# Two graph layers on one core: joined first stage, other chunks in the middle and at the end, another order inside a pair of groups

## The chip, the cores and the metric

The kernel runs on one core of one Trainium2 chip. The metric is the device time of one launch in microseconds (us). A core has a matrix engine (PE), a vector engine (DVE), an activation engine (ACT), GpSimd (POOL), which here mainly issues gathers and scatters by index, and SyncE (SP), which here only issues plain transfers. They run their own instruction lists and meet by semaphores.

## The reference

N = 3125 nodes with 256 features, E = 50000 edges sorted by `dst`, 128 features and one weight for each edge. Cut to what matters:

```python
h = concat(x[src], x[dst])                       # layer 0, an MLP on each edge
h = tanh(h @ W0 + b0); h = tanh(h @ W1 + b1); h = h @ W2 + b2
h = h * (edge_attr @ Wg)
x = layernorm(x + segment_sum(h, src) / max(segment_count(src), 1))

h = einsum('ni,hio->hno', x, W)                  # layer 1, 4 heads of 64
e = leaky_relu(a_src.h[src] + a_dst.h[dst], 0.2) * edge_weight
p = exp(e - max(e)); alpha = p / (segment_sum(p, dst)[dst] + 1e-10)
x = layernorm(x + segment_sum(h[src] * alpha, dst))
```

## The kernel before

Nodes lie in 25 tiles of 128. Edges lie in 391 blocks of 128, 98 groups of 4 blocks and 49 pairs of 2 groups. Since edges are sorted by `dst`, the receivers of a group lie in one window of 128 nodes. Products of the first layer are made of a high and a low part, three matmuls for each (L1420 to L1422). The launch has five stages, and the semaphores and the order in which each engine's function is written set the order of everything.

**First stage.** PE makes x·W0 for 25 "sender" tiles and then 25 "receiver" tiles (`node_part`, 6 matmuls each, 8 banks). DVE adds the bias to a sender tile into the ring `stA` of 4 slots (L573), and SP stores it to the table TA in HBM (L1164). For a receiver tile ACT copies the high part into the ring `stB` (L1698), DVE writes the low part (L539), and SP stores both to TB (L1169). A sender tile has 203 KB, a receiver tile 406 KB. POOL gathers rows of TA when all of TA is written. Between the sender tiles DVE makes the low parts of the weights. `wait_stage_n0` lets DVE, ACT and SP go on when all products are made and all stores have landed. Then SP loads the receiver rows of windows 0 and 1 (`load_window`: `rel`, then TW out of TB in two halves), DVE clears some constants (L721 to L725) and makes the first one-hot matrix (`window_hot`, L647).

**Group loop.** For each of the 98 groups PE runs the whole edge MLP and the sums of a block's edges by sender; ACT does tanh and copies; DVE low parts and one-hot matrices; POOL gathers TA and adds rows to four tables accA in HBM (L1316). At each step SP issues window g+2, then `ef` (edge features) and `bcast_i` (sender numbers) of g.

**Middle.** When the adds have landed (`wait_stage_a`), SP loads the four tables in five chunks of 5 tiles (`tab`, two buffers). DVE sums them and makes the mean, the residual and the statistics (`mean_residual`), ACT takes the root and normalises (`deviations`, `normalise`), PE transposes and multiplies by the weights Wc, whose last columns are a product of WcT and `ablk` (L1567). ACT copies a tile's result in two parts, `node` and `hst` (L1698). SP stores `hst` to HT and `node` to DT. Behind the chunks DVE makes tables for the next stage (L810 to L828, `in_tile` among them), then waits for the last `node`.

**Pair loop.** POOL gathers rows of HT into `Hg` (L1351), 4 for a group, into a ring of 12 groups. For a pair q of two groups the work is: `edge_scores` (L875 to L897; it waits for the gathers and for PE's `destination_scores`, semaphore s_ad), `spread_maxima` (PE, L1617), `running_maximum` (L904, L908), `weighted_rows` for each group (L913, writes `xb` and frees 4 slots of `Hg`), `window_sums` for each (PE, L1628), `carry_window` (L944), `window_rows` (L860), `one_hot` (L851) and `destination_scores` (PE, 24 matmuls L1608). One turn of PE's loop before:

```python
window_sums(2 * q)
window_sums(2 * q + 1)
spread_maxima(q + 2)
destination_scores(q + 3)
```

**End.** 25 gathers by POOL bring a node's sums (`fin`). DVE and ACT do residual, statistics and normalisation in five chunks, and SP stores each tile.

Of the kernel before, what the change touches and what calls it, by code (L numbers as in the profile page):

```python
# [6 lines left out]
P = 128  # L7
# [10 lines left out]
def build_program(nc, xT, x, src_cols, dst_cols, src_row, dst_row, eT, w_cols,  # L18
# [37 lines left out]
    TC = 5  # L56
    NC = -(-NT // TC)
# [44 lines left out]
    with ctx:  # L102
# [45 lines left out]
        eps = sb("eps", [P, 1])  # L148
        zeros = sb("zeros", [P, BW])

# [17 lines left out]
        b1c = sb("b1c", [P, C2], f32, sa)  # L168
        sn = ExitStack()
# [8 lines left out]
        stA = sb("stA", [P, N0R, H0], f32, sn)  # L178
        stB = sb("stB", [P, N0R, 2, H0], f32r, sn)
# [8 lines left out]
        rel_b = sb("rel_b", [NG, GE], bf16, sn)  # L188
        W1f = sb("W1f", [P, C1, HC], f32, sn)
# [11 lines left out]
        h1s = sb("h1s", [KS, 2, GE], f32r, sa)  # L201
# [6 lines left out]
        gate = sb("gate", [P, 2, 2, OUT], f32, sa)  # L208
        mf = sb("mf", [P, 2, 2, OUT], f32, sa)
# [3 lines left out]
        EQR = 3 * BLOCKS_PER_GROUP  # L213
        eqA = sb("eqA", [P, EQR, P], f32r, sa)
        eq_low = sb("eq_low", [P, 2, P], bf16, sa)
# [17 lines left out]
        outside = sb("outside", [1, 1], i32, sc)  # L233
        in_tile = sb("in_tile", [P, NG, NT], bf16, sc)
        reached = sb("reached", [P, NT, NG], bf16, sc)
# [23 lines left out]
        TSR = 2  # L259
# [3 lines left out]
        WcT = sb("WcT", [P, DK, OUT], f32, s1)  # L263
        ablk = sb("ablk", [P, DK, 2 * HEADS], f32, s1)
        hst = sb("hst", [P, 4, BW], f32, s1)
# [123 lines left out]
        s_ldc = sem("s_ldc")  # L389
        s_tab = [sem(f"s_tab{i}") for i in range(TSR)]  # L390
# [38 lines left out]
        s_st = sem("s_st")  # L429
# [28 lines left out]

        def part_cols(i):
            return slice(i * tiles_per_part * P, min((i + 1) * tiles_per_part * P, N))  # L460
# [18 lines left out]
        def wait_stage_n0(eng):  # L479
# [4 lines left out]
            eng.wait_ge(s_rd, 16 * RDS)  # L484
            eng.wait_ge(s_pad, 16)
            eng.wait_ge(s_wl, 4)
# [6 lines left out]
        def tiles_of_chunk(c):  # L493
            return range(c * TC, min((c + 1) * TC, NT))

# [31 lines left out]
        def _(dve):  # L527
# [35 lines left out]
            def receiver_lo(t):  # L563
                n = rows_of_tile(t)
                dve.wait_ge(s_n0b, t + 1)
                lo(stB[0:n, t % N0R, 1, :], bank_n0(NT + t)[0:n, 0:H0], stB[0:n, t % N0R, 0, :]).then_inc(s_n0l, 1)

            def sender_bias(t):
                n = rows_of_tile(t)
                dve.wait_ge(s_n0, t + 1)  # L570
                if t >= N0R:
                    dve.wait_ge(s_ta[t % N0R], 16 * (t // N0R))
                dve.tensor_tensor(stA[0:n, t % N0R, :], bank_n0(t)[0:n, 0:H0], b0b[0:n, :], ALU.add)\  # L573
# [26 lines left out]
            for t in range(4):  # L600
                sender_bias(t)
# [3 lines left out]
            const(dve.tensor_scalar(low2_i[:, :, :], low_all[:, 2:4, :], 2.0, None, ALU.mult), "low_i")  # L605
# [6 lines left out]
            for t in range(4, NT):  # L612
                sender_bias(t)
                if t == 10:
# [3 lines left out]
                if t == 13:  # L618
# [9 lines left out]
                if t == 16:  # L628
                    dve.wait_ge(s_wh, 4)
                    lo(Wgl[:, :], Wgf[:, :], Wgh[:, :]).then_inc(s_wl, 1)  # L630
                if t == 20:
# [6 lines left out]
            for t in range(NT):  # L638
                receiver_lo(t)
# [80 lines left out]
            wait_stage_n0(dve)  # L720
            const(dve.memset(h2l[2 * Q:P, :, 2, :].bitcast(f32), 1.0))  # L721
            const(dve.memset(mh[:, :, :, OUT:OUT + 1].bitcast(f32), 1.0))
            const(dve.memset(mh[:, :, :, OUT + 1:AW].bitcast(f32), 0.0))
            const(dve.memset(h1s[:, :, :].bitcast(f32), 0.0))
            const(dve.memset(ml[:, :, :, OUT:AW].bitcast(f32), 0.0), "ones")  # L725

            for s in range(-2, NG + 1):
# [41 lines left out]
            def mean_residual(c):  # L769
# [5 lines left out]
                dve.tensor_tensor(rows[:, 0], rows[:, 0], rows[:, 1], ALU.add).then_inc(s_sum, 1)  # L775
                dve.wait_ge(s_sum, c + 1)
# [21 lines left out]
            wait_stage_a(dve)  # L798
            const(dve.memset(ablk[:, :, :], 0.0), "ablk")
            const(dve.memset(node[:, :, :], 0.0), "node clear")  # L800
            dve.wait_ge(s_xn, 48)
            for c in range(NC):
                mean_residual(c)
                if c >= 1:
                    norm_factors(c - 1, c - 1)
            norm_factors(NC - 1, NC - 1)

# [16 lines left out]
            const(dve.scalar_tensor_tensor(worst[:, 2:3], worst[:, 1:2], float(P), worst[:, 0:1], ALU.mult, ALU.max))  # L824
            const(dve.tensor_scalar(outside[:, :], worst[0:1, 2:3], float(P), None, ALU.is_ge), "outside")
            const(dve.memset(neg_m[:, 0:1], -LOWEST), "no maximum")
            if rows_of_block(NB - 1) < P:
                const(dve.memset(score[:, NB - 1, :], LOWEST))  # L828
            dve.wait_ge(s_hc, NT)
            const(dve.tensor_copy(iota_p, iota_row[:, :]))  # L830
# [132 lines left out]
            for q in range(-3, NQ + 1):  # L963
# [14 lines left out]
                if q + 3 < NQ:  # L978
                    one_hot(q + 3)
# [20 lines left out]
            with if_outside(dve):  # L1000
# [8 lines left out]
                dve.wait_ge(s_st, 32)  # L1009
# [77 lines left out]
            def attention_residual(c):  # L1087
# [23 lines left out]
                last.then_inc(s_att, 1)  # L1111
# [851 lines left out]
```

## Time and profile before

| | us |
|---|---|
| median of 3 runs | 2435.32 (2430.52 to 2443.21) |
| the profiled execution | 2453.26 |
| its span, first to last instruction | 2451.1 |

The profile is of one execution, 18 us above the median. Busy time is the time in which an engine works on an instruction; PE and its weight loads (PEld) overlap. Numbers in front of a row are us from the span's start. `[14.03 <-remote]` behind a row is the idle time of the engine before it and what ended that; "remote" is a releaser that the profile can't name.

### The profile page before, as it was taken

To read this page: it belongs to the slowest core of one execution; us is meant where nothing else is said; L and a number is where in the kernel's file an instruction comes from. 1 tells how busy PE (TensorE), PEld (TensorE's weight loads), DVE (VectorE), ACT (ScalarE), POOL (GpSimd) and SP (SyncE) were. 2 spreads that over 40 slices of the span, in tenths; PEclk is the share of its full clock that TensorE was granted. 3 is DMA by queue.
4 is the path that set the end of the run, shared out by engine and by line. 5 is a ranking of instruction groups with operands and counts; after the bars stand their busy time and mean duration, and the time that the engine had idled before them with its cause. 6 is when DMAs were issued, how large, how long until landed. Compare 5 with 4: busy or idle time off the path is not lost. (4 is left out here: it accounts for less than half of the span.)

```text
span 2451.1 us, 40398 instructions
## 1 busy us (share of the span) xinstructions
PE 1929.3 (79%) x12892; PEld 1704.4 (70%) x12892; DVE 1509.6 (62%) x3750; ACT 1382.8 (56%) x2780; POOL 1470.6 (60%) x1204
## 2 busy tenths in 40 slices
PE   7699999999999999999999999955134545544560
PEld 6588899988999999999999999954123333433440
DVE  6466666666666666666666666645155445444575
ACT  2488888888888888888888888845000000000012
POOL 0317778777777777767777777532645645654623
PEclk9899999999999999999999999977567667766785
DMA  5878877777777777777777777665434434444523
GB/s 198 287 204 182 196 165 169 170 166 166 160 160 158 159 159 159 157 161 154 158 159 158 158 158 159 131 158 138 107 87 120 129 106 123 129 110 109 134 83 108
DMA packets 236167, 370.81 MB, mean 151 GB/s; under 512 B 35853, under 2 KB 168935, under 8 KB 235949
## 3 DMA queue, kind: packets, MB, share of 16 engines
q0 software_dynamic: 101232, 188.20, 38.7%
q1 hardware_dynamic: 134717, 179.94, 24.4%
q8 instruction: 107, 1.75, 0.3%
q14 instruction: 111, 0.91, 0.1%
HBM read 270.57 MB, written 97.45 MB: 150 GB/s over the span
## 5 line engine op out<-in xcount | busy, mean ns | idle before, releaser
L1316 POOL DMA_INDIRECT accA<-ystage,to_a x391 | 650.2, 1663 | 231.0 <-issue 108.0
L1322 POOL DMA_INDIRECT GA<-TA,src_c x391 | 425.1, 1087 | 328.7 <-issue 93.3
L1351 POOL DMA_INDIRECT Hg<-HT,src_c x391 | 371.1, 949 | 346.0 <-DVE xb L913 168.7
L1861 ACT ACTIVATE drop<-neg_m 128x1 f32<-128x1 f32 x49 | 14.5, 295 | 627.3 <-DVE neg_m L908 517.1
L1420 PE MATMUL bank<-h1h,W1h 128*128 128x512 f32 x882 | 349.2, 396 | 1.3 <-DVE h1l L539 0.7
L1422 PE MATMUL bank<-h1h,W1l 128*128 128x512 f32 x882 | 348.0, 395 | 0.0
L1421 PE MATMUL bank<-h1l,W1h 128*128 128x512 f32 x882 | 347.0, 393 | 0.0
L539 DVE TENSOR_TENSOR h2l<-h2f,h2h 128x512 fp32r<-128x512 f32 (+1 forms) x294 | 202.8, 690 | 202.4 <-issue 87.3
L1628 PE MATMUL bank<-xb,in_window 128*128 128x260 f32 (+1 forms) x782 | 249.7, 475 | 70.3 <-issue 69.2
L539 DVE TENSOR_TENSOR h1l<-h1f,h1h 128x512 fp32r<-128x512 f32 x294 | 194.9, 690 | 131.2 <-ACT h1h L1698 112.9
L1628 PEld LDWEIGHTS bank<-xb,in_window 128*128 128x128 f32 (+1 forms) x782 | 182.4, 241 | 122.4 <-issue 87.3
L1698 ACT ACTIVATE mh<-mf 128x512 fp32r<-128x512 f32 x196 | 123.9, 632 | 207.5 <-DVE mf L676 195.1
L1617 PE MATMUL bank<-diag,ones 128*128 128x128 f32 x98 | 27.5, 371 | 249.5 <-DVE diag L897 180.1
L1421 PE MATMUL bank<-W2l,h2h 128*128 128x256 f32 (+1 forms) x782 | 220.9, 282 | 0.0
L1420 PE MATMUL bank<-W2h,h2h 128*128 128x256 f32 (+1 forms) x782 | 219.7, 281 | 0.4 <-DVE mf L676 0.4
L1422 PE MATMUL bank<-W2h,h2l 128*128 128x256 f32 (+1 forms) x782 | 219.4, 281 | 0.0
L1729 ACT ACTIVATE h1f<-bank 128x512 f32<-128x512 f32 (+1 forms) x392 | 206.9, 584 | 10.1 <-PE bank L1472 10.1
L1754 ACT ACTIVATE h2f<-bank,b1c 128x512 f32<-128x512 f32 x294 | 201.9, 687 | 6.7 <-issue 1.3
L1617 PEld LDWEIGHTS bank<-diag,ones 128*128 128x128 f32 x98 | 20.7, 239 | 261.3 <-DVE diag L897 188.3
L1422 PEld LDWEIGHTS bank<-h1h,W1l 128*128 128x128 f32 x882 | 165.8, 188 | 39.3
L1420 PEld LDWEIGHTS bank<-h1h,W1h 128*128 128x128 f32 x882 | 166.5, 189 | 36.6 <-DVE h1l L539 3.4
L875 DVE TENSOR_TENSOR score<-Hg,bank 128x32 f32<-128x32 f32 (+2 forms) x50 | 9.0, 182 | 295.4 <-remote 286.4
(209 smaller groups left out, 5235.1 us busy)
## 6 DMA issues: line engine op xcount, KB each, us to landing
TW<-TB SPq DMA_DIRECT2D x196, 203.0 KB
ef<-in_eT SPq DMA_DIRECT2D x97, 256.0 KB
bcast_i<-in_src_row SPq DMA_DIRECT2D x97, 256.0 KB
HB<-hist SPq DMA_DIRECT2D x98, 130.0 KB
rel<-RL SPq DMA_DIRECT2D x97, 128.0 KB
rem<-RD SPq DMA_DIRECT2D x48, 256.0 KB
TB<-stB SPq DMA_DIRECT2D x24, 406.0 KB
accA<-zeros SPq DMA_DIRECT2D x4, 1677.0 KB, 13.0
```

The lines of the kernel that those rows point to most:

```text
L539: return dve.tensor_tensor(o, full, hi.bitcast(f32), ALU.subtract)
L1316: return pool.indirect_dma_start(out=table, out_offset=bass.IndirectOffsetOnAxis(ap=rows, axis=0), in_=sums, in_offset=None, compute_op=AL ...
L1322: pool.indirect_dma_start(out=GA[0:n, b % (GAR * BLOCKS_PER_GROUP), :].bitcast(f32), out_offset=None, in_=TA, in_offset=bass.IndirectOffse ...
L1351: pool.indirect_dma_start(out=Hg[0:n, slot, :], out_offset=None, in_=HT, in_offset=bass.IndirectOffsetOnAxis(ap=src_c[0:n, b:b + 1], axis= ...
L1420: pe.matmul(o, lh, rh, start=first, stop=False)
L1421: pe.matmul(o, lh, rl, start=False, stop=False)
L1422: return pe.matmul(o, ll, rh, start=False, stop=last)
L1617: pe.matmul(PTOP[:, 0:P], ones[:, :], diag[:, q % 2, :], start=True, stop=True).then_inc(s_sp, 1)
L1628: last = pe.matmul(PS[g % 3][:, 0:BW], in_window[0:n, j, :], xb[0:n, j, :], start=b == blocks[0], stop=b == blocks[-1])
L1698: return act.activation(o, i, ACT.Copy)
L1729: act.activation(h1f[0:k1(c), c, 0:n], PT[u % 2][0:k1(c), 0:n], ACT.Tanh).then_inc(s_tanh1, 1)
L1754: act.activation(h2f[:, m, 0:n], PL1[u % 2][:, 0:n], ACT.Tanh, bias=b1c[:, m:m + 1]).then_inc(s_tanh2, 1)
```

## The change

**First stage.** A list `STEPS` mixes the tiles: at each 7 steps two receivers to five senders until the senders are done (25 senders and 10 receivers in the first 35 steps), then the other 15 receivers. PE, DVE, ACT and SP follow it. SP loads window 0 behind step 35, once the first ten receiver tiles have landed, and window 1 behind step 37; the rows that these two windows ask for are clamped to the first ten tiles, and a test at the end covers other inputs. The wait for the stores leaves the start of the group loop: DVE and ACT pass it at s = 1, SP ahead of window 2.

**Group loop.** SP issues `ef` and `bcast_i` of g ahead of window g+2. At g = 14 it loads WcT and `ablk`.

**Middle and end.** Chunks of 3, 5, 5, 5, 5 and 2 tiles; three buffers `tab`; `in_tile` and the other tables ahead of the chunks; the product WcT·ablk right behind the group loop; ACT's table of the root loaded ahead of the wait (`warm`); 20 matmuls of `ident` on PE when the first tables land; `hst` takes all 264 columns and POOL copies `node` out of it (25 copies), no store to DT; the factors of chunk c-1 are made inside chunk c; ACT takes the roots of c+1 behind two thirds of a chunk in the middle, and at the end behind the normalisation of c.

**Pair loop.** `edge_scores(q + 2)` and `spread_maxima(q + 2)` move between the pair's two groups, and `one_hot` ahead of `window_rows`.

```diff
+        EARLY = 10
+        steps_s, steps_r, STEPS = [], [], []
+        while len(STEPS) < 2 * NT:
+            sender = len(steps_s) < NT and len(STEPS) % 7 not in (1, 4)
+            (steps_s if sender else steps_r).append(len(STEPS))
+            STEPS.append(("sender" if sender else "receiver", len(steps_s if sender else steps_r) - 1))
...
-            wait_stage_n0(dve)
...
-            for s in range(-2, NG + 1):
+            window_hot(0)
+            wait_products_n0(dve)
+            const(dve.memset(h2l[2 * Q:P, :, 2, :].bitcast(f32), 1.0), "ones")
+            const(dve.memset(ablk[:, :, :], 0.0), "ablk")
+
+            for s in range(-1, NG + 1):
+                if s == 1:
+                    wait_stores_n0(dve)
...
-            wait_stage_n0(sp)
-            load_window(0)
-            load_window(1)
+                if p == 35:
+
+                    for k in range(N0R):
+                        sp.wait_ge(s_tb[k], early_stores(k))
+                    sp.wait_ge(s_xl, PARTS)
+                    sp.wait_ge(s_rd, 16 * RDS)
+                    load_window(0)
+                if p == 37:
+                    load_window(1)
+            wait_products_n0(sp)
             for g in range(NG):
                 n = edges_of_group(g)
-                if g + 2 < NG:
-                    load_window(g + 2)
...
+                if g + 2 < NG:
+                    load_window(g + 2)
...
-    TC = 5
-    NC = -(-NT // TC)
+
+    CHUNKS = [range(a, b) for a, b in zip((0, 3, 8, 13, 18, 23), (3, 8, 13, 18, 23, NT))]
...
-            copy(node[0:n, t, :], bank[t % 4][0:n, BW:BW + HEADS])
-            copy(hst[0:n, t % 4, :], bank[t % 4][0:n, 0:BW]).then_inc(s_hc, 1)
+                act.wait_ge(s_nd, t - 3)
+            copy(hst[0:n, t % 4, :], bank[t % 4][0:n, 0:BW + HEADS]).then_inc(s_hc, 1)
...
+            pe.wait_ge(s_tab[0], chunk_arrivals(0))
+            for _ in range(20):
+                pe.matmul(bank[3][:, 0:P], ident[:, :], ident[:, :], start=True, stop=True)
...
+                if 0 <= q + 2 < NQ:
+                    edge_scores(q + 2)
                 if 0 <= q < NQ:
                     weighted_rows(2 * q + 1)
                 if 0 <= q - 1:
                     carry_window(2 * q - 1)
-                if 0 <= q + 2 < NQ:
-                    edge_scores(q + 2)
+                if q + 3 < NQ:
+                    one_hot(q + 3)
```

On PE in the pair loop, from the third turn on, before:

```order
L1628 MATMUL bank<-xb,in_window 128x260 x8
L1617 MATMUL bank<-diag,ones 128x128
L1608 MATMUL bank<-ad_p,hot 128x4 x24
L1628 MATMUL bank<-xb,in_window 128x260 x8
L1617 MATMUL bank<-diag,ones 128x128
```

and now (L1694 is the line that was L1628, L1683 was L1617, L1674 was L1608):

```order
L1694 MATMUL bank<-xb,in_window 128x260 x4
L1683 MATMUL bank<-diag,ones 128x128
L1694 MATMUL bank<-xb,in_window 128x260 x4
L1674 MATMUL bank<-ad_p,hot 128x4 x24
L1694 MATMUL bank<-xb,in_window 128x260 x4
```

The maxima's matmul stands between the two groups' sums; the destination scores stay behind the second.

On DVE in the same loop, from a pair's first `weighted_rows` on, before:

```order
L913 TENSOR_TENSOR xb<-Hg,bank3 128x4x256
L932 TENSOR_TENSOR drop_k<-drop,keep 128x1
L944 SCALAR_TENSOR_TENSOR hist<-hist,drop_k,bank7 128x260
L904 TENSOR_REDUCE top_g<-bank1 128x1
L908 SCALAR_TENSOR_TENSOR neg_m<-top_g,neg_m 128x1
L913 TENSOR_TENSOR xb<-Hg,bank3 128x4x256
L944 SCALAR_TENSOR_TENSOR hist<-hist,keep,bank5 128x260
L875 TENSOR_TENSOR score<-Hg,bank0 128x32
L883 SCALAR_TENSOR_TENSOR score<-score 128x32
L889 TENSOR_TENSOR score<-score,w_c 128x32
L892 TENSOR_REDUCE top_c<-score 128x1
L897 TENSOR_SCALAR diag<-ident,top_c 128x128
```

and now (L958 was L913, L920 to L942 were L875 to L897, L896 was L851, L905 was L860):

```order
L958 TENSOR_TENSOR xb<-Hg,bank3 128x4x256
L977 TENSOR_TENSOR drop_k<-drop,keep 128x1
L989 SCALAR_TENSOR_TENSOR hist<-hist,drop_k,bank5 128x260
L949 TENSOR_REDUCE top_g<-bank1 128x1
L953 SCALAR_TENSOR_TENSOR neg_m<-top_g,neg_m 128x1
L920 TENSOR_TENSOR score<-Hg,bank0 128x32
L928 SCALAR_TENSOR_TENSOR score<-score 128x32
L934 TENSOR_TENSOR score<-score,w_c 128x32
L937 TENSOR_REDUCE top_c<-score 128x1
L942 TENSOR_SCALAR diag<-ident,top_c 128x128
L958 TENSOR_TENSOR xb<-Hg,bank3 128x4x256
L989 SCALAR_TENSOR_TENSOR hist<-hist,keep,bank6 128x260
```

The five score instructions stand ahead of the second `xb` instead of behind its carry.

On SP behind the row stores of the first stage, before:

```order
L1158 DMA RL<-rel_b 1x336
L1164 DMA TA<-stA 128x406 x24
L1164 DMA TA<-stA 48x406
L1164 DMA TA<-stA 5x406
L1169 DMA TB<-stB 128x812 x24
L1169 DMA TB<-stB 48x812
L1169 DMA TB<-stB 5x812
L1182 DMA rel<-RL 128x512
```

and now, at the end of the mixed tiles (L1228 stores senders, L1232 receivers, L1215 and L1221 load a window):

```order
L1228 DMA TA<-stA 5x406
L1232 DMA TB<-stB 128x812
L1215 DMA rel<-RL 128x512
L1218 TENSOR_LOAD low_i
L1218 ISA x2
L1221 ISA
L1221 DMA TW<-TB 128x406
```

The first window's loads stand 14 receiver tiles ahead of the end of the stores.

## Rows read from the trace of the kernel before

**Rows 1.** The page: busy time, share of the span, instructions.
```profile
PE 1929.3 (79%) x12892; PEld 1704.4 (70%) x12892; DVE 1509.6 (62%) x3750; ACT 1382.8 (56%) x2780; POOL 1470.6 (60%) x1204
```

**Rows 2.** Windows, group loop and pair loop: from:to, length, busy by engine (instructions), clock, DMA share, GB/s.
```profile
104.40:1608.00 1503.60, 1500.69 (x10245) 1360.69 (x10246) 1033.38 (x2617) 1259.64 (x2421) 1044.22 (x756) 1.00 0.74 163
1698.60:2387.00 688.40, 308.74 (x2053) 238.14 (x2053) 334.49 (x745) 38.63 (x153) 371.10 (x391) 0.69 0.43 114
```

**Rows 3.** Windows inside the first stage, same columns.
```profile
30.00:60.00 30.00, 27.32 (x138) 25.96 (x136) 20.18 (x42) 6.20 (x14) 0.00 (x0) 0.94 0.50 177
60.00:95.00 35.00, 25.62 (x118) 22.85 (x117) 11.99 (x21) 10.17 (x20) 15.31 (x16) 0.90 0.97 354
```

**Rows 4.** First stage, waits of ACT, 30 to 105 us: total, times, longest.
```profile
ACT stB L1698 <- DMA TB<-stB: 14.0, 13, 4.2
```

**Rows 5.** First stage, timeline of DVE and PE.
```profile
99.46 0.91 DVE L721 MEMSET h2l<- 64x1024 f32 x1 [3.13 <-DMA TB<-stB]
104.38 0.79 PE L1472 MATMUL bank<-hot,TW 128*128 128x256 f32 x2 [13.62 <-DMA TW<-TB]
```

**Rows 6.** Group loop, timeline of SP's queue and DVE.
```profile
820.78 0.42 SPq L1182 DMA_DIRECT2D rel<-RL  x1
823.82 0.55 DVE L647 TENSOR_SCALAR hot<-rel,half_f 128x512 fp32r<-128x512 bf16 x1
```

**Rows 7.** Middle, timeline of DVE, PE, ACT and POOL.
```profile
1644.67 1.50 DVE L775 TENSOR_TENSOR tab<-tab 128x1290 f32<-128x1290 f32 x1 [6.14 <-DMA tab<-accA]
1647.87 0.60 SPq L1228 DMA_DIRECT2D ablk<-in_a_dst  x1
1651.96 1.85 PE L1567 MATMUL bank<-ablk,WcT 128*128 128x8 f32 x8 [25.61 <-DMA ablk<-in_a_dst]
1655.42 0.30 ACT L1831 ACTIVATE std<-mv,eps 128x5 f32<-128x5 f32 x1
1696.10 0.17 ACT L1698 ACTIVATE node<-bank 53x4 f32<-53x4 f32 x1 [0.57 <-PE bank L1588]
1696.17 0.37 ACT L1698 ACTIVATE hst<-bank 53x260 f32<-53x260 f32 x1
1698.62 1.02 POOL L1351 DMA_INDIRECT Hg<-HT,src_c  x1 [62.31 <-DMA HT<-hst]
```

**Rows 8.** Pair loop, 1698.6 to 2387 us: waits of DVE and POOL.
```profile
DVE score L875 <- remote: 286.4, 22, 47.3
POOL Hg L1351 <- DVE xb L913: 168.7, 23, 16.1
```

**Rows 9.** Pair loop, timeline of DVE, POOL and PE around one restart.
```profile
2017.90 0.19 DVE L875 TENSOR_TENSOR score<-Hg,bank 128x32 f32<-128x32 f32 x1 [14.03 <-remote]
2020.52 1.21 DVE L913 TENSOR_TENSOR xb<-Hg,bank 128x1024 f32<-128x1024 f32 x1
2022.00 0.94 POOL L1351 DMA_INDIRECT Hg<-HT,src_c  x1 [7.33 <-DVE xb L913]
2028.54 0.75 PE L1608 MATMUL bank<-ad_p,hot 128*128 128x4 bf16 x24
2040.73 0.95 POOL L1351 DMA_INDIRECT Hg<-HT,src_c  x1 [0.30 <-issue]
2044.89 0.19 DVE L875 TENSOR_TENSOR score<-Hg,bank 128x32 f32<-128x32 f32 x1 [14.04 <-remote]
```

**Rows 10.** Pair loop, timeline of PE and DVE where POOL does not pause.
```profile
1884.14 0.19 DVE L875 TENSOR_TENSOR score<-Hg,bank 128x32 f32<-128x32 f32 x1 [14.04 <-remote]
1893.41 0.75 PE L1608 MATMUL bank<-ad_p,hot 128*128 128x4 bf16 x24
1905.12 0.19 DVE L875 TENSOR_TENSOR score<-Hg,bank 128x32 f32<-128x32 f32 x1 [3.84 <-remote]
1969.68 0.18 DVE L875 TENSOR_TENSOR score<-Hg,bank 128x32 f32<-128x32 f32 x1
```

**Rows 11.** End, timeline of ACT.
```profile
2443.92 5.02 ACT L1837 ACTIVATE xn<-xn,shift,rstd 128x256 f32<-128x256 f32 x10
```

More of the change, by code:

```diff
@@ L262, in build_program @@
         x1T = sb("x1T", [P, XTR, DK, P], f32, s1)
-        WcT = sb("WcT", [P, DK, OUT], f32, s1)
-        ablk = sb("ablk", [P, DK, 2 * HEADS], f32, s1)
-        hst = sb("hst", [P, 4, BW], f32, s1)
+        hst = sb("hst", [P, 4, BW + HEADS], f32, s1)
         s1.close()
@@ L457, in build_program, with early_stores @@
         part_of_tile = [t // tiles_per_part for t in range(NT)]
+        EARLY = 10
[4 more added lines that the diff above has]
+            STEPS.append(("sender" if sender else "receiver", len(steps_s if sender else steps_r) - 1))
+        def early_stores(slot):
+            return 16 * sum(len(pieces(t)) for t in range(slot, EARLY, N0R))
         def part_cols(i):
@@ L493, in tiles_of_chunk @@
         def tiles_of_chunk(c):
[L494 removed]
+            return CHUNKS[c]
         def load_tables(eng, chunks):
@@ L599, in _, with staged @@
             dve.wait_ge(s_b0, 16)
-            for t in range(4):
-                sender_bias(t)
+            def staged(p):
+                kind, t = STEPS[p]
+                if kind == "sender":
+                    sender_bias(t)
+                else:
+                    receiver_lo(t)
+            for p in range(4):
+                staged(p)
             dve.wait_ge(s_lowp, 1)
@@ L796, in norm_factors @@
                     .then_inc(s_shift, 1)
[L798 to L806, printed above, removed]
+            dve.wait_ge(s_Yc, NB)
             low = low_all[:, 0, :]
@@ L828, in _ @@
                 const(dve.memset(score[:, NB - 1, :], LOWEST))
+            wait_stage_a(dve)
+            const(dve.memset(node[:, :, :], 0.0), "node clear")
+            dve.wait_ge(s_xn, 48)
+            for c in range(NC):
+                mean_residual(c)
+            norm_factors(NC - 1, NC - 1)
             dve.wait_ge(s_hc, NT)
+            dve.wait_ge(s_nd, NT)
             const(dve.tensor_copy(iota_p, iota_row[:, :]))
@@ L1205, in _ @@
                              src_row[g * GE:g * GE + n].partition_broadcast(P)).then_inc(s_bc[g % 2], 16)
+                if g == 0:
+                    for k in range(N0R):
+                        sp.wait_ge(s_tb[k], stores(N0R, k))
+                    sp.wait_ge(s_pad, 16)
+                if g + 2 < NG:
+                    load_window(g + 2)
                 if g in (2, 3):
@@ L1353, in gather_h_rows @@
                     in_offset=bass.IndirectOffsetOnAxis(ap=src_c[0:n, b:b + 1], axis=0)).then_inc(landed, 16)
+            pool.wait_ge(s_dc, DC["node clear"])
+            for t in range(NT):
+                n = rows_of_tile(t)
+                pool.wait_ge(s_hc, t + 1)
+                pool.tensor_copy(node[0:n, t, :], hst[0:n, t % 4, BW:BW + HEADS]).then_inc(s_nd, 1)
+            pool.wait_ge(s_nd, NT)
             for k in range(4):
@@ L1425, in node_part @@
             def node_part(u):
-                t, half = u % NT, u // NT
+                kind, t = STEPS[u]
+                half = 0 if kind == "sender" else 1
                 n = rows_of_tile(t)
@@ L1704, in _, with receiver_hi @@
                 copy(xTh[:, :, part_cols(i)], xTf[:, :, part_cols(i)]).then_inc(s_xh, 1)
+            def receiver_hi(t):
+                n = rows_of_tile(t)
+                act.wait_ge(s_n0, steps_r[t] + 1)
+                if t >= N0R:
+                    act.wait_ge(s_tb[t % N0R], 16 * (t // N0R))
+                copy(stB[0:n, t % N0R, 0, :], bank_n0(steps_r[t])[0:n, 0:H0]).then_inc(s_n0b, 1)
+            for t in range(6):
+                receiver_hi(t)
             act.wait_ge(s_ldw, 16 * (C1 + 2 * 2 + 2 * 3 + 2 + 2 + 1))
@@ L1716, in _ @@
             copy(Wgh[:, :], Wgf[:, :]).then_inc(s_wh, 1)
[L1717 to L1722 removed]
+            for t in range(6, NT):
+                receiver_hi(t)
             def tanh1(g, c):
```

193 lines of the change are left out of this document (104 added, 89 removed).

## The prediction

> **What bounds the kernel now.** The page's busy shares [rows 1] name no single engine: PE is busy for 79% of the span, POOL 60%, DVE 62%. So the windows come next [rows 2], and then, stage by stage, the table of waits and the timeline around the longest of them. In the group loop PE is busy 1500.7 of 1503.6 us at full clock: PE alone sets 61% of the span, and nothing that the change does to the other engines there can gain. The other stages have 947 us. In the longest of them, the pair loop, the busiest engine (POOL) works 371 of 688 us. There engines wait for each other, and the waits are what the change can move. The times below are differences of stages in the profiled execution (2453.3 us, of which 2451.1 is span). That run lies 18 us above the median, which no stage owns visibly, so I take the sum of the differences off the median, 2435.3. What a measurement of this kernel can tell from no change is about 0.5%, 12 us.
>
> **First stage.** The transfers are the bound, unevenly: from 30 to 60 us, the senders' half, they move 177 GB/s at a DMA share of 0.50, and from 60 to 95 us 354 GB/s at 0.97 [rows 3]. There ACT waits 14 us for slots of `stB` [rows 4]. Behind it stands a tail: stores landed at 99.46, windows loaded, PE's first matmul of the loop at 104.38 after 13.6 us of idleness [rows 5].
> Mixing the tiles fills the first half. 30 x 177 + 35 x 354 KB per us = 17.7 MB; all at 354 GB/s is 50 us, so 15 us less. PE allows it: 138 matmuls in 27.3 us [rows 3] are 0.198 us each, a step of six 1.19 us, 50 steps 59 us; with the first at about 22 they end near 82. Last low part then about 84, h2l's clearing 0.9 (the other clearings of 99.46 to 102 move off the path), and PE starts the group near 87 to 90. Window 0 is loaded 15 steps, some 18 us, earlier; only the wait for all stores (now ahead of window 2, first needed two groups or 30 us later) stays, hidden by PE's two groups. The gain by the end of the products is 104.4 - 88.5 = 16; by the transfers 15. Against: POOL's gathers of TA start later, since the last sender is now step 34 instead of 24, and share the transfers with the last receivers. Bounds: 10 (the first gathers late by 5 us) to 19. I take **-15**.
>
> **Group loop.** PE's work is the same, so **0**. The one thing that moves towards the path is `rel`: SP issued it a turn (15 us) earlier, and now issues it behind `bcast_i`, which waits for DVE's duplicates. In the old trace that place is 820.78, and `window_hot` used it at 823.82 [rows 6]: 3.0 us, 0.42 of it the issue. DVE has 31% of idle time in this loop [rows 2], so a microsecond's delay is absorbed; above that it costs up to 1 us x 96 groups. WcT and `ablk`, nine loads of 0.60 us each in SP's queue [rows 7] (one stands there), now delay one turn of SP by about 6 us, once; a turn lasts 15.3 us (1503.6 / 98) and the loads then behind them are due a turn later.
>
> **Middle.** The first root stands at 1655.42, though DVE started on the tables at 1644.67: ACT had to wait for the product of Wc, and that for `ablk`, the last of whose eight loads SP queued at 1647.87: the product ran from 1651.96 for 1.85 us [rows 7]. With both made during the group loop and a first chunk of three tiles (3/5 of the table bytes and of the statistics; my estimate for these, from the sum's 1.50 us for five tiles, is 4 us from the sum's start to the root instead of 6) the first root comes near 1648: -7.5. From there to the last `hst` (1696.54) are 41.1 us for 25 tiles. Dropping `node` (0.07 us until `hst` starts, 0.17 by its own duration [rows 7]) gives 2 to 4 us, a last chunk of two tiles and the later place of the roots 1 or 2 more. POOL's 25 copies run beside ACT; ACT's pace is 41.1/25 = 1.64 us a tile, and only a copy slower than that would show: at 2 us, 25 x 0.36 = +9. `in_tile` and its neighbours now precede the chunks, while the last adds and the tables are under way: DVE waited 6.14 us for the tables alone [rows 7], about what they take, so nothing either way. The store to DT stood behind the last `hst`, on no path. The 20 dummy matmuls stand where PE waits. Sum **-12**, bounds -3 and -16.
>
> **End.** ACT's last piece normalises ten tiles, 5.02 us [rows 11]; the root of the last chunk stood ahead of the normalisation of the one before. With two tiles left it is 2 x 0.5: -4. The first chunk of three can start up to 2 gathers (2.5 us) earlier, of which I count 1. **-5**, bounds -2 and -8.
>
> **Pair loop.** 688 us, 14.0 a pair. POOL's own work is 371 us [rows 2], so it isn't the bound; it waits 169 us for `xb`, and DVE waits 286 us in 22 pieces ahead of `edge_scores` for something the profile calls remote [rows 8]. Around one piece [rows 9]: restart of DVE at R = 2017.90, two `xb` free the ring, POOL restarts at 2022.00 and issues 16 gathers without a pause, the last at 2040.73 for 0.95 us, DVE restarts at 2044.89. A ring of 12 groups has the gathers landed long before. What `edge_scores` otherwise waits for is s_ad, the signal of PE's destination scores. Those ran at 2028.54, for 0.75 us, and DVE went on only 15.6 us later, 3.2 us behind the end of POOL's row of gathers. So I read: **signals of PE are held back while POOL issues gathers in a long row.** The cycle is 27.0 us for two pairs: 4.1 (R to POOL) + 19.7 (16 gathers) + 3.2.
> The change alters both ends. After R DVE does the scores (1.1 us) and then at once the second `xb` (1.21), instead of scores, `window_rows` (1.22), `one_hot`, `xb` [rows 9]: POOL restarts at about R + 2.5, 1.6 earlier. If still two pairs fit in a cycle, it is 25.4 us. 18 cycles of 27.0 us are 486 of the 688 us; the rest is the start (one wait of 47.3 us [rows 8]), the stretch of rows 10 and the end. So 18 x 1.6 = -29, bounds 0 and -35 (22 waits).
> But PE's destination scores of the next pair now stand behind the second group's sums, which need that second `xb`: R + 2.3, 8 matmuls of L1628, about 3.3 (an estimate: PE's 308.7 us of the stage [rows 2] are 6.3 us a pair, most of it the sums of two groups), and 0.75 for the scores: R + 6.3, nearly 4 us into POOL's row. Before they were done ahead of POOL's restart, and their signal passed. Rows 10 show one such case: scores at 1893.41 in the middle of a row, DVE's restart at 1905.12.
> The Trainium skill (SBUF — State Buffer, the section on SBUF's two separate sides) says that only the port pair shared by DVE and GpSimd causes contention, and that PE and ACT never wait for anyone. By that rule nothing holds PE's signals; it would give rival D's second value, 2235. The trace speaks against it: in the 14.04 us ahead of 2044.89 DVE is idle and has no port to share, and still the signal doesn't come.
>
> **Rivals.**
> (A) Two pairs per cycle, restart earlier, all terms as above: -15 - 12 - 5 - 29 = -61, **2374**. For it: the mechanism's first half is read off directly. Chance 0.36.
> (B) The pair loop doesn't change, since the signal is released at a fixed time of its own: -32, 2403. Chance 0.17.
> (C) The signal is held at every pair: only two `xb` are free in a cycle, so POOL has 8 gathers: 2.5 + 9.7 + 3.2 = 15.4 us a pair instead of 13.5, times 48 is +91, in all 2494; with the 11 us of rows 10 now and then only, +30, 2433. It is slower than before from about 14.2 us a pair on. For it: rows 10. Against: in the stretch from 1884.14 to 1969.68 [rows 10], where POOL hardly pauses and such cases occur, seven pairs took 85.5 us, 12.2 each. Chance 0.24, 0.14 of it slower than before.
> (D) That stretch's 12.2 us a pair become the rule, since POOL no longer pauses: -1.3 x 48 = -62, 2341; with no signal held at all POOL is the bound, 8 x 1.25 = 10 us a pair (the 16 gathers of rows 9 in 19.7 us), -3.5 x 48 = -168, 2235. Chance 0.18, nearly all at the first value.
> (E) `rel` comes late in the group loop, +0.5 to +1 us each, or the mixed stage loses what it wins: 2435 to 2480. Chance 0.05.
>
> **How the numbers follow.** The likeliest is A, 2374. The range leaves out the worst half of C and of E and the tail of D: 2325 to 2450. Faster by over 0.5% (below 2423): A, B, D and 0.06 of C and E, 0.77. Within: 0.07. Slower (above 2447): 0.16.
>
> **What would show it.** First stage: PE's first one-hot matmul (was L1472) near 88, and a DMA share near 1 from 35 us on; if it is at 95 or later, the gathers of TA were late. Group loop: 1503 us long, no wait for `rel`. Middle: the first root 4 us behind the start of the first table sum instead of 11, and POOL's first gather of `Hg` 12 us nearer to the group loop's end. Pair loop: DVE's remote waits still about 22 with POOL's restart 2.5 us behind each (A); about 45 waits, each after 8 gathers (C); few waits and PE's scores passing during the row (D). End: last normalisation of two tiles. The forecast is wrong if the held signals turn out to be something else, such as gathers that land late: then the order inside a pair decides nothing, and B comes.

## The result, and the profile after

The changed kernel takes 2396.57 us (median of 4 runs, 2395.63 to 2399.12); the kernel before 2432.92 us (4 runs, 2429.91 to 2443.21). The ratio is 0.9855, with a 95% interval of 0.9832 to 0.9878: 36 us faster, inside the stated range, where 61 us were forecast. The profiled run of after took 2397.3 us, next to its median, while that of before lay 18 us above its own. A stage's difference between these two profiles is therefore too large, and a second profile of before (2431.96 us, span 2429.7) stands beside them in this table. Its columns are the start of PE's group loop, the loop to POOL's last add, from there to the first gather of `Hg`, from there to the first gather of `fin`, and the rest.

| kernel | loop starts | group loop | middle | pair loop | end |
|---|---|---|---|---|---|
| before | 104.4 | 1530.5 | 63.8 | 696.1 | 56.3 |
| before, second profile | 102.8 | 1526.1 | 62.9 | 682.5 | 55.4 |
| after | 94.5 | 1523.9 | 57.6 | 664.3 | 55.4 |

Against the second profile the stages give -8.3, -2.2, -5.3, -18.2 and 0: 34 us, about the difference of the medians. The forecast had -15, 0, -12, -29 and -5. No stage got slower; each gain but the group loop's was overrated.

The windows of after by stage, with the columns of [rows 2]:

```profile
94.50:1608.00 1513.50, 1512.25 (x10365) 1378.79 (x10365) 1040.58 (x2648) 1266.58 (x2446) 1049.10 (x761) 1.00 0.74 164
1676.00:2340.30 664.30, 336.36 (x2053) 255.73 (x2053) 341.03 (x746) 38.85 (x153) 374.85 (x392) 0.71 0.46 118
```

PE still fills the group loop (its idleness fell from 2.9 to 1.3 us), and the pair loop is still one in which everyone waits.

**First stage**, timeline of ACT, DVE and PE, in order of engine; the last row answers to the last of [rows 5]:

```profile
73.34 0.51 ACT L1765 ACTIVATE stB<-bank 128x406 fp32r<-128x406 f32 x1 [5.95 <-DMA TB<-stB]
80.70 0.51 ACT L1765 ACTIVATE stB<-bank 128x406 fp32r<-128x406 f32 x1 [5.86 <-DMA TB<-stB]
...
93.41 0.57 DVE L563 TENSOR_TENSOR stB<-bank,stB 53x406 fp32r<-53x406 f32 x1 [1.04 <-ACT stB L1765]
93.91 0.47 DVE L686 TENSOR_SCALAR hot<-rel,half_f 128x512 fp32r<-128x512 bf16 x1
...
94.52 0.76 PE L1532 MATMUL bank<-hot,TW 128*128 128x256 f32 x2 [9.32 <-DVE hot L686]
```

The last low part comes at 93.41, not at 84. Until 65 us PE was the limit, as reckoned: it worked all of the 35 us from 30 to 65. From there on it was not. PE stood 9.3 us in front of the first one-hot matrix, which DVE makes behind the last receiver tile. ACT waited twice for nearly 6 us for slots of `stB`, between 67 and 81 us; POOL issued its 16 gathers of TA from 65.3 to 86.0.

**Middle**, timeline of DVE, ACT and POOL; the rows answer to [rows 7]:

```profile
1626.37 0.97 DVE L817 TENSOR_TENSOR tab<-tab 128x774 f32<-128x774 f32 x1 [4.36 <-DMA tab<-accA]
...
1630.38 0.30 ACT L1909 ACTIVATE std<-mv,eps 128x3 f32<-128x3 f32 x1 [19.28 <-DVE mv L809]
1633.03 1.58 ACT L1915 ACTIVATE xn<-xn,shift,rstd 128x256 f32<-128x256 f32 x3 [2.35 <-DVE shift L839]
...
1637.42 0.30 ACT L1909 ACTIVATE std<-mv,eps 128x5 f32<-128x5 f32 x1 [2.27 <-DVE mv L809]
...
1673.14 0.38 ACT L1765 ACTIVATE hst<-bank 53x264 f32<-53x264 f32 x1 [0.64 <-PE bank L1650]
...
1676.00 1.03 POOL L1403 DMA_INDIRECT Hg<-HT,src_c  x1 [2.24 <-DMA HT<-hst]
```

The first root stands 4.0 us behind the first table sum, where it was 10.8. From the first root to the last `hst` it is 42.8 us, where it was 40.8.

**Pair loop**, waits of DVE and POOL from 1676 to 2340 us; they answer to [rows 8]:

```profile
DVE score L920 <- remote: 285.8, 37, 27.0
...
POOL Hg L1403 <- DVE xb L958: 138.9, 42, 10.6
```

And one turn of its timeline, of POOL, DVE and PE; it answers to [rows 9]:

```profile
1910.59 0.95 POOL L1403 DMA_INDIRECT Hg<-HT,src_c  x1 [2.74 <-DVE xb L958]
...
1919.39 0.95 POOL L1403 DMA_INDIRECT Hg<-HT,src_c  x1 [0.30 <-issue]
...
1908.01 0.19 DVE L920 TENSOR_TENSOR score<-Hg,bank 128x32 f32<-128x32 f32 x1 [5.95 <-remote]
...
1909.11 1.21 DVE L958 TENSOR_TENSOR xb<-Hg,bank 128x1024 f32<-128x1024 f32 x1
...
1920.50 0.19 DVE L920 TENSOR_TENSOR score<-Hg,bank 128x32 f32<-128x32 f32 x1 [5.95 <-remote]
...
1914.02 0.83 PE L1674 MATMUL bank<-ad_p,hot 128*128 128x4 bf16 x24
```

DVE restarts at R = 1908.01, POOL at R + 2.58, PE's destination scores run at R + 6.0, POOL's row of 8 gathers ends at 1920.34, and DVE goes on at 1920.50. So one pair takes 12.5 us, and nearly every pair waits: 37 waits for 49 pairs instead of 22. Before, two pairs took 27.0 us with one wait.

The waits go with POOL's gathers. Its last gather of `Hg` ends at 2297.1, and from 2298 on the last pairs take 6.5 us each with no remote wait. The longest wait stands behind the longest row, 52 gathers from 1676.00 to 1741.18 (timeline of PE, DVE and POOL):

```profile
1716.74 0.83 PE L1674 MATMUL bank<-ad_p,hot 128*128 128x4 bf16 x24
...
1749.16 0.19 DVE L920 TENSOR_TENSOR score<-Hg,bank 128x32 f32<-128x32 f32 x1 [27.01 <-remote]
...
1740.23 0.95 POOL L1403 DMA_INDIRECT Hg<-HT,src_c  x1 [0.30 <-issue]
```

Here DVE goes on 31.6 us behind the end of PE's scores, and 8.0 us behind the end of POOL's row.

### The profile page after: what moved, and what is told of

Its sections match the earlier page's. It is cut to its first block and busy times, and to the rows that moved or that the text cites. A ratio compares the mean times of both kernels' runs of the same rounds, so it can differ in the third digit from the quotient of the medians.

```text
span 2395.7 us, 40504 instructions
## 1 busy us (share of the span) xinstructions
PE 1951.7 (81%) x12932; PEld 1726.8 (72%) x12932; DVE 1510.6 (63%) x3765; ACT 1377.7 (58%) x2758; POOL 1479.6 (62%) x1229
## 5 line engine op out<-in xcount | busy, mean ns | idle before, releaser
L1368 POOL DMA_INDIRECT accA<-ystage,to_a x391 | 653.8, 1672 | 246.4 <-DMA accA<-ystage,to_a 117.7
L1374 POOL DMA_INDIRECT GA<-TA,src_c x391 | 419.8, 1074 | 298.7 <-issue 99.3
L1694 PE MATMUL bank<-xb,in_window 128*128 128x260 f32 (+1 forms) x782 | 280.0, 519 | 48.0 <-issue 47.6
L1694 PEld LDWEIGHTS bank<-xb,in_window 128*128 128x128 f32 (+1 forms) x782 | 195.0, 262 | 96.1 <-issue 58.8
L1683 PE MATMUL bank<-diag,ones 128*128 128x128 f32 x98 | 34.1, 446 | 267.1 <-DVE diag L942 147.0
L1683 PEld LDWEIGHTS bank<-diag,ones 128*128 128x128 f32 x98 | 23.2, 283 | 285.5 <-DVE diag L942 154.7
L920 DVE TENSOR_TENSOR score<-Hg,bank 128x32 f32<-128x32 f32 (+2 forms) x50 | 9.2, 187 | 294.8 <-remote 285.8
L1765 ACT ACTIVATE h2h<-h2f 128x512 fp32r<-128x512 f32 x294 | 185.4, 631 | 9.3
```

Of the source, the lines that this page charges most:

```text
L1368: return pool.indirect_dma_start(out=table, out_offset=bass.IndirectOffsetOnAxis(ap=rows, axis=0), in_=sums, in_offset=None, compute_op=AL ...
L1374: pool.indirect_dma_start(out=GA[0:n, b % (GAR * BLOCKS_PER_GROUP), :].bitcast(f32), out_offset=None, in_=TA, in_offset=bass.IndirectOffse ...
L1694: last = pe.matmul(PS[g % 3][:, 0:BW], in_window[0:n, j, :], xb[0:n, j, :], start=b == blocks[0], stop=b == blocks[-1])
L1765: return act.activation(o, i, ACT.Copy)
```

## The experiments

The kernels of a set run on one chip beside the kernel before. There were three sets, and their chips fall into two kinds; this turned out to be the key. On two chips of the first kind the kernel before takes 2428 us, and its 2433 us in the result are of that kind too; on the one chip of the second kind it takes 2256.75 us (2254.43 to 2261.11, 19 runs).

**The kernel before again** (no edit).

> The kernel before, unchanged, for a second profile of it: the profiled run of before was 18 us above the median of its runs, that of after within 1 us of its own. If the 18 us lie in the pair loop, the first gather of Hg (was 1698.62) stays within 3 us and the first gather of fin (was 2394.75) comes at about 2377; then the pair loop's true gain is about 14 us instead of the 31.8 that the two profiles give. If they are spread over the whole run, both move in proportion (12 and 17 us).

2431.96 us in one run. The timeline of POOL, first gather of `Hg` and first gather of `fin`:

```profile
1691.79 1.02 POOL L1351 DMA_INDIRECT Hg<-HT,src_c  x1 [61.44 <-DMA HT<-hst]
...
2374.26 0.95 POOL L1411 DMA_INDIRECT fin<-HB,row_i  x1 [41.07 <-issue]
```

The pair loop took 682.5 us instead of 696.1, and 6.8 us more went missing ahead of it. The pattern is the same: 22 remote waits, and 26.8 us for two pairs instead of 27.0. But the stretches without long waits (pairs of 12 to 13 us) lie elsewhere and are of other lengths. Of the 21 us between these two executions 14 lie in the pair loop.

**SP's order in the group loop put back** in the changed kernel:

```diff
                 n = edges_of_group(g)
+                if g >= 1 and g + 2 < NG:
+                    load_window(g + 2)
                 if g >= 2:
                     sp.wait_ge(s_eh, g - 1)
```

(and the load behind `bcast_i` stays for g = 0 alone)

> The changed kernel with SP's order in the group loop put back (window g+2 ahead of ef and bcast of g, from g = 1 on). Theory: that order let ef land late, and the 6.8 us by which the group loop shrank between groups 2 and 34 came from the new order; then this kernel is 5 to 8 us slower than the changed one (2396.6 to about 2403), with waits of ACT for ef of some 14 us in the first 500 us of the loop. Rival: the loop was shorter since it started without the backlog of the first stage; then the time stays within 2 us of 2396.6.

2396.0 us (2394.83 to 2397.61), where the changed kernel took 2396.57 on its own chip: no difference that the medians show. In ACT's waits from 104 to 600 us those for `ef` are back, and the changed kernel has none:

```profile
ACT eh L1766 <- DMA ef<-in_eT: 9.3, 13, 1.8
```

The loop in the profile was 3.9 us longer (1527.8), but the loop began 1.4 us earlier, and the pair loop took 2.2 less. That is not chance: the eight profiled kernels with SP's new order and 16 gathers ahead took 1523.7 to 1525.5 us, those with the old order and the old first stage 1526.1 to 1530.5. So the order is worth some 2 to 4 us of the loop, of a wait that PE's work mostly covers; in the medians it is lost.

**The old order of the pair loop in the changed kernel**, twice, on two chips of the first kind:

```diff
+                if 0 <= q < NQ:
+                    weighted_rows(2 * q + 1)
+                if 0 <= q - 1:
+                    carry_window(2 * q - 1)
                 if 0 <= q + 2 < NQ:
                     edge_scores(q + 2)
-                if 0 <= q < NQ:
-                    weighted_rows(2 * q + 1)
-                if 0 <= q - 1:
-                    carry_window(2 * q - 1)
```

(and on DVE `one_hot` again behind `window_rows`, on PE both groups' sums again ahead of the maxima).

> The changed kernel with the pair loop's order of before on DVE and PE. If the order gives what the two profiles show, 2396.6 + 32 = 2428; if most of that was the slow profiled run of before, 2396.6 + 14 = 2411, restarts of DVE again 27 us apart for two pairs, and first fin gather 14 us later after the first Hg gather than the 664.3 us of after.

> The changed kernel with the old order of the pair loop, again. Theory (the order counts only where PE's signals are held): on the second chip within 3 us of after_again; on the first chip 10 us above it. Rival (the order shortens DVE's own path everywhere): 10 us above it on either.

2406.47 us (2402.84 to 2409.55) beside 2396.0 of the kernel above, which equals the changed one; and 2404.25 (2398.66 to 2407.22) beside 2394.19 (2390.20 to 2397.19) of the changed kernel, run again on the same chip. Both times the new order is worth 10 us, with no overlap of the single runs. The pair loop's length was 672.2 and 675.4 us against 664.3 and 663.7, and two pairs took 26.8 us again.

> The changed kernel once more, for a comparison with the next three on one chip. The runs so far fall into two groups: on one chip the kernel before takes 2428 to 2433 us, on another 2257, and there a pair takes 10.0 us (POOL's 8 gathers) in every version. If this is the second chip, theory: the pair loop is POOL's there and only the first stage and the middle count, so 2257 - 9 - 6 = 2242 to 2247; if it is the first, 2396 again.

**Only the new order of the pair loop**, in the kernel before:

> The kernel before with only the new order of the pair loop. By the same two theories 2433 - 32 = 2401 or 2433 - 14 = 2419; one restart of DVE for each pair, 12.5 us apart, POOL issuing 8 gathers in a row. The first stage, group loop and middle as before (first gather of Hg near 1698).

2415.13 us (2411.02 to 2418.68) beside 2428.23 (2415.76 to 2435.72) of the kernel before, ratio 0.9951 (0.9919 to 0.9982): 13 us, and by the interval 4 to 20. The pair loop took 661.7 us, with 37 waits, as in the changed kernel; all else was as before. So the order alone gives 10 to 13 us, and the -32 of the first two profiles and even the -18 of the better pair contain the spread of the old kernel's pair loop.

**Without the destination scores** of 48 of 49 pairs, on both kinds of chip:

```diff
-                dve.wait_ge(s_ad, q + 1)
+                dve.wait_ge(s_ad, 1)
...
-                if q + 3 < NQ:
+                if q + 3 < 1:
                     destination_scores(q + 3)
```

(and `one_hot` without its wait for s_ad; this part of the result is then missing)

> The changed kernel with PE's destination scores left out for all pairs but the first (48 of 49 times 24 matmuls L1674; their result of pair 0 serves all pairs, so this part of the computation is missing) and no wait for s_ad behind the first. Theory (edge_scores waits for the signal of the destination scores, held while POOL issues a row of gathers): the 36 waits of 6 us ahead of the scores vanish, and either the next held signal of PE (s_S ahead of hist or in_window, s_sp ahead of top_g) takes their place, then a pair keeps at 12 to 13 us, or none does and POOL's 10 us a pair is the bound, 12.5 - 10 = 2.5 us x 45 = 110 us faster, about 2285. Rival (edge_scores waits for gathers that land late): the waits stay where they are, ahead of the scores, 6 us each, and the time stays near 2396.

> The changed kernel without the destination scores of 48 of the 49 pairs and without the wait for them (that part of the computation is missing), again. On the second chip as before, 2244. On the first chip, theory (held signal of the destination scores): the waits of 6 us ahead of the scores go, and the time falls by up to 110 us, or a held signal of another step takes over at 12 to 13 us a pair; rival (gathers that land late there): the waits ahead of the scores stay and the time is 2396.

The first of these ran on the chip of the second kind: 2243.95 us (2241.84 to 2246.05), with a pair loop as long as the others' there. The second ran on one of the first kind: 2360.72 us (2358.76 to 2362.69), 33 us faster than the changed kernel beside it. There DVE's waits from 1680 to 2300 us read

```profile
DVE hist L987 <- remote: 191.9, 17, 14.7
DVE score L918 <- DMA Hg<-HT,src_c: 26.4, 4, 8.7
```

The remote waits ahead of the scores are gone. Late gathers would have left them where they were, since the scores still wait for the gathers: what is left is the first four pairs' waits, which end with the landing, and these scores start 10.1 us apart (at 1690.1, 1700.2, 1710.3 and 1720.4), where the changed kernel's started 27 and 34 us apart. Another wait took their place, ahead of `hist`, which waits for s_S, the signal behind PE's sums. The timeline of DVE, ACT and PE at one of them:

```profile
1908.16 0.48 DVE L987 SCALAR_TENSOR_TENSOR hist<-hist,keep,bank 128x260 f32<-128x260 f32 x1 [11.42 <-remote]
...
1920.08 0.48 DVE L987 SCALAR_TENSOR_TENSOR hist<-hist,drop_k,bank 128x260 f32<-128x260 f32 x1 [8.70 <-remote]
...
1908.16 0.29 ACT L1945 ACTIVATE bank<-score,neg_m 128x32 f32<-128x32 f32 x1 [13.35 <-remote]
...
1890.36 1.99 PE L1692 MATMUL bank<-xb,in_window 128*128 128x260 f32 x8 [0.59 <-issue]
...
1896.84 1.99 PE L1692 MATMUL bank<-xb,in_window 128*128 128x260 f32 x8 [0.58 <-issue]
1911.41 3.80 PE L1692 MATMUL bank<-xb,in_window 128*128 128x260 f32 x8 [12.58 <-issue]
```

PE had no sums running between 1898.83 and 1911.41. What the `hist` at 1908.16 waited for was therefore done by 1898.83, and its signal came at least 9.3 us late, while POOL issued gathers all along (by the kernel's order it was the sums of 1890.36, which end 15.8 us before). `hist` also waits for the store of an older `hist` to land, so that might be what was late. But ACT goes on in the same moment, and what it waited for there is the same value of s_S and no store. So what is late is PE's signal, whichever it is: two engines that wait for it get it together. Signals to PE pass meanwhile: its maxima at 1895.77 start 0.05 us behind the end of DVE's `diag`, in the same row of gathers.

This settles the first half of what the prediction read from rows: it is signals that are late, not gathers. That POOL's rows hold them is shown below by the four gathers. When a held signal is let go isn't shown: behind rows of 8, 16 and 52 gathers it came 0.16, 3.2 and 8.0 us after the end, and at 1908.16 it came in the middle of a row. Nor is it the signals alone. In the kernel before PE's destination scores sometimes come one matmul at a time, though nothing between them waits (timeline of PE, around the end of the row of gathers that [rows 10] show):

```profile
1907.88 0.53 PE L1608 MATMUL bank<-ad_p,hot 128*128 128x4 bf16 x15 [1.04 <-DVE hot L851]
1910.66 0.16 PE L1608 MATMUL bank<-ad_p,hot 128*128 128x4 bf16 x1 [2.25 <-issue]
...
1917.66 0.28 PE L1608 MATMUL bank<-ad_p,hot 128*128 128x4 bf16 x5 [0.54 <-issue]
```

There are 24 such gaps in its pair loop, 30.6 us, and none in the changed kernel. Why the chip does all this, no run here shows.

**POOL at most 6 groups ahead** in the changed kernel (`if g >= 6: pool.wait_ge(s_xb, g - 6 + 1)`):

> The changed kernel where POOL may be at most 6 groups ahead of the weighted rows instead of 12: the first row of gathers is 24 long instead of 48 (30 us instead of 60). Theory (signals held during a row): the first waits of DVE, 24 and 27 us in the changed kernel, shrink by some 25 to 30 us in all, and the steady cycle stays at 12.5 us, so about 2370. Rival (late gathers): with the gathers issued later the waits ahead of the scores get longer, above 6 us, and the kernel gets slower.

It ran on the chip of the second kind, so its question stays open: 2258.87 us (2257.75 to 2261.03, 10 runs) beside 2256.75 of the kernel before. There its pair loop took 537.2 us, against 520 to 521 of the three other kernels on that chip, with 12 groups. Nothing is held there (DVE has no remote wait in any of the four kernels), and a shorter ring only makes POOL wait (22.2 us for `xb`, where the kernel below waits 3.7).

**Four gathers first** in the first stage (`if ahead == 1: pool.wait_ge(s_n0l, NT)` in POOL's loop), on both kinds:

> The changed kernel where POOL gathers only the 4 blocks of group 0 ahead of the last receiver tile and the other 12 behind it. In the changed kernel the 16 gathers ran from 65.3 to 86.0 us, and in that time DVE's receiver tiles stood still twice for 5 us. Theory: the row of gathers (by its transfers or by held signals) delays the receivers; then PE's first one-hot matmul comes at 85 to 88 instead of 94.5 and the kernel gains up to 8 us, less what group 1 to 3 wait for their gathers. Rival: the receivers are slow because their stores fill the transfers anyway; then the first matmul stays within 2 us of 94.5.

> The changed kernel with only the first 4 gathers of the first stage ahead of the last receiver tile, again, now beside the changed kernel on the same chip. Theory: PE's first one-hot matmul 4 to 5 us earlier (89 instead of 93 to 94.5) and the kernel 3 to 5 us faster than after_again on either chip; rival: what is gained at the start is lost in groups 1 to 3, which wait for their gathers, and the time is that of after_again.

Second kind: 2241.90 us (2240.05 to 2244.32), with PE's loop starting at 89.1, and at 92.7 to 94.7 in the three other kernels on that chip. First kind: 2403.93 (2399.53 to 2404.26), ten us slower than the changed kernel beside it, though its loop starts at 88.7 (timeline of PE, then ACT):

```profile
88.73 0.77 PE L1534 MATMUL bank<-hot,TW 128*128 128x256 f32 x2 [5.81 <-DVE hot L686]
...
110.37 0.75 PE L1525 MATMUL bank<-ident_r,GA 128*128 128x128 f32 x4 [7.41 <-ACT h1f L1804]
...
98.01 0.47 PE L1534 MATMUL bank<-hot,TW 128*128 128x256 f32 x2
...
109.72 0.60 ACT L1804 ACTIVATE h1f<-bank 128x512 f32<-128x512 f32 x1 [7.20 <-remote]
```

The loop then took 1537.1 us instead of 1523.9. POOL's gathers that were put off now ran in one row from 88.5 to 108.6, beside the first groups, and PE waited 7.4 us for ACT, which itself waited for PE: the product that its `h1f` needs ended at 98.48, and ACT went on at 109.72, 1.1 us behind the row. The same kernel on the second kind has such a row too, but its product ends at 98.69 and its `h1f` starts at 98.72, and the loop takes 1525.2 us. The changed kernel has no such row and no remote wait there. So on the first kind of chip a row of gathers that is put elsewhere brings the late signal with it: this is the experiment that ties the two together.

The timeline and waits of this kernel on the second kind show what the pair loop is when no signal is held (waits of all engines, 1672 to 2192 us, then DVE):

```profile
DVE score L920 <- DMA Hg<-HT,src_c: 155.2, 42, 8.7
...
POOL Hg L1405 <- issue: 115.2, 378, 0.3
...
1909.60 0.19 DVE L920 TENSOR_TENSOR score<-Hg,bank 128x32 f32<-128x32 f32 x1 [3.40 <-DMA Hg<-HT,src_c]
```

POOL issues a gather each 1.25 us without a pause, a pair takes 10.2 us on average, and DVE waits for the gather itself: the profile can name that releaser, and it is not "remote".

**Pauses between the last gathers**: POOL waits for a chunk's gathers of `fin` before it issues the next chunk's.

> The changed kernel where POOL, at the end, waits for a chunk's gathers of fin to land (2.7 us) before it issues the next chunk's. In the changed kernel DVE stood still for short pieces between 2363 and 2375 while POOL issued 25 gathers in a row, and the end took as long as before (55.4 us). Theory (held signals): with rows of at most 5 gathers DVE runs through, the last chunk's gathers land some 13 us later than now (at 44 of 55 us), and the end takes 48 to 52 us: 3 to 7 us faster. Rival: DVE's pieces have another cause, then the later gathers make the end 0 to 5 us longer.

Second kind of chip: 2252.50 us (2249.26 to 2254.35). The end took 54.8 us, and 46.0 in the three other kernels on that chip. The pause costs 8.8 us where nothing is held. On the first kind it wasn't tried. But these kernels show what the held signals cost there: the same end takes 54.8 to 55.8 us on chips of the first kind.

## Why the prediction was right or wrong

**First stage: right in mechanism, mis-sized (-15 against -8 to -10).** The step that failed is the end of the products, "near 82", and the last low part "about 84". From 65 us on PE's rate was not the limit: `stB` was, with two waits of 5.95 and 5.86 us. I had put the late gathers down as a risk for their own landing; what they did was to stand in the receivers' way. The experiment with four gathers gives the size: the loop starts at 88.7 and 89.1, my 88.5. The delay is the same on both kinds of chip (92.7 to 94.7 with 16 gathers), and from 65 to 86 us the DMA share is 0.97 with 16 gathers and 0.86 to 0.88 with 4. Both speak for shared transfers and against held signals.

**Group loop: 0 against -2 to -7 in the profiles.** `rel` was not late, as expected. I had not priced that `ef` comes earlier, which took away ACT's waits (13.9 us before); by the experiment that is 2 to 4 us of the loop, and below what the medians can tell.

**Middle: -12 against -5 to -6.** The first term held: counted from POOL's last add, the first root came 20.6 us later before and 12.0 now, -8.6 where -7.5 stood. The second term had the wrong sign: -4 was forecast behind the first root, +2 came. ACT started early and then waited 2.35 us for DVE's factors, which now stand behind the next chunk's table sum, and 2.27 us for the next chunk's statistics. Starting one engine of a chain early moves its wait behind the start. POOL's copies were hidden (0.19 us each in the median, and 47 us of waiting between them).

**End: -5 against 0 to -1.** The two terms were there: the first chunk starts 5.2 us behind the first gather instead of 7.8, and the last piece of ACT is 1.09 us instead of 5.02 [rows 11]. What I left out is that DVE's own signals are held too while POOL issues 25 gathers in a row. The timeline of DVE in after:

```profile
2368.58 0.18 DVE L809 BATCH_NORM_AGGREGATE mv<-stats 128x2 f32<-128x6 f32 x1 [0.52 <-remote]
2369.28 0.18 DVE L809 BATCH_NORM_AGGREGATE mv<-stats 128x2 f32<-128x6 f32 x1 [0.52 <-remote]
2369.98 0.18 DVE L809 BATCH_NORM_AGGREGATE mv<-stats 128x2 f32<-128x6 f32 x1 [0.52 <-remote]
2370.08 0.14 DVE L1139 TENSOR_TENSOR cden<-fin,scale 128x20 f32<-128x20 f32 x1
2373.50 0.18 DVE L1141 TENSOR_SCALAR cden<-cden 128x20 f32<-128x20 f32 x1 [3.28 <-remote]
2374.88 0.28 DVE L1143 RECIPROCAL cinv<-cden 128x20 f32<-128x20 f32 x1 [1.20 <-DVE cden L1141]
```

`cden` at 2373.50 waits only for the instruction of 2370.08, DVE's own, and ACT's root of the statistics of 2369.98 starts at 2373.47: again two engines go on together, 2.1 us behind POOL's last gather. What was won ahead of POOL's row was lost in it; from its end on it takes 24.3 us, where it took 25.4 before.

**Pair loop: right sign and half of the mechanism, wrong cycle (-29 against -10 to -13).** The step that failed is "if still two pairs fit in a cycle". POOL's restart came at R + 2.58 (2.5 was forecast) and the destination scores at R + 6.0 (6.3). But not two pairs fit in a cycle, as in A: the scores run inside POOL's row and are held at every pair, which is rival C's pattern, 37 waits. Its price was wrong. I had taken 3.2 us from the end of the row to DVE's restart from [rows 9]. There the row is 16 gathers long; behind a row of 8 it is 0.16 us. So 2.58 + 9.75 + 0.16 = 12.5 us a pair instead of 15.4, a little below the old 13.4. The saving was also counted for 18 cycles, and in the trace of before only 14 waits have the full 14 us. Rival D, 12.2 us a pair, came near in the time of a pair with another reason. The gain is small because the change trades one long wait for two of half its length. The part that the order can't touch is the start: DVE waited 24.5 and 27 us in and behind POOL's first row, which fills the ring.

**The rule of the Trainium skill** (SBUF — State Buffer, two separate sides) that PE waits for no one was set against the trace. What the prediction drew from it, that nothing holds PE's signals, fails on chips of the first kind: they are late by up to 31.6 us. The rule itself is about ports to SBUF, and no run here shows a wait for a port, so it is neither borne out nor refuted. On the second kind a pair takes 10.2 us, near the 10 that rival D gave with no signal held.

**The sum.** 36 us came where 61 were forecast. The range of 125 us holds A, B, D's first value and part of C, so that the time fell into it says little. The nearest figure is rival B's, 2403 us, and that is luck: B has the pair loop unchanged, and both experiments with the old order show that it did change. The spread of the old kernel's pair loop, 682 to 696 us in two profiles, was larger than I allowed for when I took the differences of stages off the median.

## What to carry to other kernels

A wait whose releaser the profile can't name is worth an experiment that takes the waited-for work away: if another wait of like length takes its place, it is the signals that are late, and reordering single instructions gains only a part. Where one engine issues gathers in a long row, put what the others must hear ahead of the row or count on its end and some us more; and run the kernel before on each chip, since what holds on one may not on the next. Before costing a stage from one profile, look at how much that stage varies between two.

## What was not expected of the hardware

The kernel before takes 2257 us on one chip and 2428 on two others. It has no profile on the fast one; in the changed kernel's versions with 12 groups nearly all of the difference is the pair loop (520 to 521 against 662 to 664 us) and the end (46.0 against 55.4), while the first stage, the group loop and the middle agree within 3 us, the group loop with four gathers first apart. Behind a row of 8 gathers the held signals came 0.16 us after its end, behind one of 16 gathers 3.2 us, behind one of 52 8.0 us. Whether the changed kernel is faster on a chip of the second kind wasn't run; the kernel with four gathers first is there, 2241.9 against 2256.75 us (ratio 0.9936, 0.9919 to 0.9952). An estimate for the changed kernel itself is 2243 us, 14 us less than before: the 2252.5 of the kernel with pauses less their 8.8 us, or the 2258.9 of the shorter ring less the 16 by which its pair loop is longer. That is about what the first stage, the group loop and the middle gave on the first kind (16 us).
